# Turning the quantised 1024-wide activations by a DMA transpose in place of eight TensorE transposes and a ScalarE copy

## The reference

```
h  = layernorm(x);  q = h Wq;  k, v = split(concat(ctx, h) Wkv)     # 16 heads of 16, 1101 keys
x1 = x + softmax(mask(q k^T / 4)) v Wout + bout                      # query i sees keys up to i + 77
g  = layernorm(x1)
a  = gelu(quant(g) quant(w_fc)^T + b_fc)                             # 256 -> 1024
out = x1 + quant(a) quant(w_proj)^T + b_proj                         # 1024 -> 256
```

## Time and profile before

| | |
|---|---|
| Median of 3 runs | 743.06 us (741.91 to 748.08) |
| Profiled execution, its own time | 746.14 us |
| Its span, first to last instruction | 744.4 us |
| Mean granted clock of PE, of full speed | 0.924 |
| PE / ACT / DVE / POOL busy | 615.4 / 461.5 / 417.2 / 209.3 us |
| 16 DMA engines, hardware queue | 42.6% of the span, 42.63 MB |

### The profile page before, as it was taken

The page is one execution under the profiler, slowest core; times in us unless marked ns, Lnnn a source line. Parts: engine busy times, 40 slices in busy tenths (PEclk is TensorE's granted clock), DMA queues, the critical chain, the costliest instruction groups (busy, mean ns, idle before and its releaser), DMA issues.

```text
span 744.4 us, 11509 instructions
## 1 busy us (share of the span) xinstructions
PE 615.4 (83%) x4031; PEld 260.7 (35%) x4040; DVE 417.2 (56%) x888; ACT 461.5 (62%) x612; POOL 209.3 (28%) x272
## 2 busy tenths in 40 slices
PE   3668876869989888798899879898899879998365
PEld 2333323223345324323444324333344324233223
DVE  3321567685643846827654756537426658572664
ACT  2335745457855677587765775587775767888022
POOL 2202322142122541232423532133331532232100
PEclk9969979799999999999999999899999999999756
DMA  5495691444039590207239570108069540100000
GB/s 141 52 110 112 73 145 13 146 50 44 1 49 121 67 94 22 90 2 80 41 46 109 74 66 16 44 1 92 30 67 111 77 39 17 44 3 29 0 0 29
DMA packets 43911, 43.64 MB, mean 59 GB/s; under 512 B 3979, under 2 KB 43527, under 8 KB 43834
## 3 DMA queue, kind: packets, MB, share of 16 engines
q1 hardware_dynamic: 43834, 42.63, 42.6%
HBM read 12.12 MB, written 4.19 MB: 22 GB/s over the span
## 4 chain that ended last, share of the span: by engine, by line
PE 64%; ACT 14%; DVE 10%; issue 8%; DMA 2%; SPq 1%; DVEq 0%; POOL 0%; ACTq 0%
PE psO L1166 18%; PE psS L1181 14%; ACT probs L662 9%; PE psD L1044 9%; PE psD L1054 5%; PE psD L1078 4%; PE psD L1113 4%; PE psD L1098 4%; PE psD L1096 2%; PE psD L1104 2%; ACT hT L692 1%; DMA k_stack<-k_parts 1%; DVE amax L813 1%; DVE stats L776 1%; DVE hid L824 1%
## 5 line engine op out<-in xcount | busy, mean ns | idle before, releaser
L662 ACT ACTIVATE probs<-psS 128x1024 f32<-128x1024 f32 (+3 forms) x384 | 330.6, 909 | 190.9 <-PE psS L1181 190.1
L1181 PE MATMUL psS<-q_stack,k_stack 99*128 99x512 bf16 (+4 forms) x896 | 198.6, 334 | 47.6 <-ACT probs L662 43.4
L607 POOL TENSOR_SCALAR_AFFINE_SELECT probs<-probs 128x512 f32<-128x512 f32 (+2 forms) x160 | 109.6, 696 | 333.4 <-ACT probs L662 333.3
L1166 PE MATMUL psO<-probs,v_aug 128*17 128x512 f32 (+4 forms) x1792 | 182.6, 506 | 1.1 <-issue 0.8
L1181 PEld LDWEIGHTS psS<-q_stack,k_stack 99*128 99x128 bf16 (+1 forms) x896 | 70.6, 103 | 168.0 <-ACT probs L662 116.7
L1166 PEld LDWEIGHTS psO<-probs,v_aug 128*17 128x17 f32 (+1 forms) x1792 | 37.3, 98 | 93.7 <-issue 82.0
L813 DVE TENSOR_REDUCE amax<-hid 128x32 f32<-128x1024 f32 x44 | 53.3, 1210 | 29.2 <-ACT hid L747 28.6
L939 DVE STREAM_TRANSPOSE o_cols<-psO 128x512 f32<-128x512 f32 x32 | 22.9, 717 | 75.1 <-PE psO L1166 74.8
L747 ACT ACTIVATE hid<-psD 128x512 f32<-128x512 f32 x64 | 36.8, 597 | 40.7 <-PE psD L1098 40.5
L824 DVE TENSOR_TENSOR hid<-hid,magic 128x1024 f32<-128x1024 f32 x44 | 56.9, 1292 | 4.6 <-issue 3.8
L825 DVE TENSOR_TENSOR hq<-hid,magic 128x1024 bf16<-128x1024 f32 x40 | 54.6, 1366 | 1.4
(11 more groups left out here) (88 smaller groups left out, 584.0 us busy)
## 6 DMA issues: line engine op xcount, KB each, us to landing
q_stack<-q_parts SPq DMA_DIRECT2D x96, 128.0 KB, 8.3
k_stack<-k_parts SPq DMA_DIRECT2D x48, 147.2 KB, 8.4
k_stack<-k_parts SPq DMA_DIRECT2D x48, 128.0 KB, 9.5
x_in<-in_x_dram SPq DMA_DIRECT2D x8, 512.0 KB, 6.5
x<-in_x_dram SPq DMA_DIRECT2D x8, 512.0 KB, 8.7
out_dram<-x SPq DMA_DIRECT2D x16, 256.0 KB, 2.2
hid<-in_L_ffn_w_fc_dram SPq DMA_DIRECT2D x1, 1024.0 KB, 14.4
hid<-in_L_ffn_w_proj_dram SPq DMA_DIRECT2D x1, 1024.0 KB, 5.0
```

Of the source, the lines that this page charges most:

```text
L607: last = pool.affine_select(out=tile, in_=tile, compare_op=ALU.is_ge, fill=0.0, base=first - (P * t - CTX), pattern=[[0, GH], [1, m]], cha ...
L662: act.activation(probs[:, k % PB, 2 * pair:2 * pair + 2, 0:n], psS[:, 2 * pair:2 * pair + 2, 0:n], ACT.Exp, scale=DH ** -0.5).then_inc(pro ...
L1166: last = pe.matmul(psO[SQ * j:SQ * j + VW, first - CHUNK * st.c:first - CHUNK * st.c + n], v_aug[0:rows, v_tile(st.b, st.c, t), GH * st.g ...
L1181: last = pe.matmul(psS[0:rows, j, off:off + n], k_stack[0:ROWS, GH * st.g + j, P * t:P * t + rows], q_heads(0, ROWS, st)[:, j, first - CHU ...
```

## The change

For each token tile the kernel no longer does the eight PE transposes and the ACT copy; SP issues one DMA transpose, 128x1024 bf16 from `hq[:, t % 2]` to `hT[:, t % 2]`, SBUF to SBUF. `hT` leaves `IN_BANK` and `BY_ACT`, so it takes no bank and the turns of the others shift. SP waits for `hq_ready`, and from the third tile on for PE having finished the `proj` that read the buffer. The waits of DVE's `hq` and PE's `proj` on the turned tile become waits on the DMA's semaphore (`turned`). In the bursts `hT` is placed a half or a whole slot after its `hq` (some a slot earlier than before), and the second `proj` of most bursts a slot later. The context load, until now inside `xin` and so waiting for `ctxT` of the batch before, becomes an item of its own, `cin`, at slot -42.

```
--- before.py
+++ after.py
@@ -172,6 +172,7 @@
         if b:
             put(b, (-45, -68, -81)[b - 1], "xin", b, 0)
             put(b, (-44.5, -67.5, -80.5)[b - 1], "xin", b, 1)
+            put(b, -42, "cin", b)
             for c, places in enumerate((((-35, -34, -33), (-32, -30, -29)), ((-65, -63, -61), ), ((-54, -52, -51), ))[b - 1]):
                 for s, kind in zip(places, ("ln1", "ln1root", "ln1end")):
                     put(b, s, kind, b, c)
@@ -209,11 +210,11 @@
                 put(b, s, kind, b, c)
             series(b, [places[2] + 1 + t for t in range(SUB)], "x1b", b, SUB * c)
         if not b:
-            burst(put, b, 0, 36, (39, 40, 42, 43, 44, 45, 46, 47), (41.5, 43.5, 46.5, 48.5), (46, 49.5))
+            burst(put, b, 0, 36, (39, 40, 42, 43, 44, 45, 46, 47), (40.5, 43.5, 46.5, 47.5), (46, 49.5))
         else:
-            burst(put, b, 0, 28, (31, 32, 34, 35, 36, 37, 38, 39), (33.5, 36.5, 38.5, 40.5), (38, 42))
+            burst(put, b, 0, 28, (31, 32, 34, 35, 36, 37, 38, 39), (32.5, 35.5, 38.5, 39.5), (38, 43))
         if b < B - 1:
-            burst(put, b, 1, PER_BATCH + 11, (14, 15, 16, 18, 19, 20, 21, 22), (16.5, 19.5, 21.5, 23.5), (21, 25))
+            burst(put, b, 1, PER_BATCH + 11, (14, 15, 16, 18, 19, 20, 21, 22), (15.5, 18.5, 21.5, 22.5), (21, 26))
     for i in range(2):
         for h in range(2):
             put(0, 21 + 9 * i + 2 * h - i * h, "wquant", i, h)
@@ -251,8 +252,8 @@
 
 PLAN = plan()
 ORDER = [it for k in range(-1, TOTAL + 1) for h in (0, 1) for it in PLAN[k, h]]
-IN_BANK = ("wout", "xqT", "fc", "hT", "proj", "ctxT", "xnT", "qk", "v", "flag", "wT")
-BY_ACT = ("ctxT", "xnT", "v", "hT")
+IN_BANK = ("wout", "xqT", "fc", "proj", "ctxT", "xnT", "qk", "v", "flag", "wT")
+BY_ACT = ("ctxT", "xnT", "v")
 
 
 def act_plan():
@@ -419,6 +420,7 @@
         x1_read = sem("x1_read")
         x1_biased = sem("x1_biased")
         xq_ready = sem("xq_ready")
+        hT_loaded = [sem("hT_loaded0"), sem("hT_loaded1")]
         hq_ready = sem("hq_ready")
         y_stored = [sem(f"y_stored{i}") for i in range(CHUNKS)]
 
@@ -443,6 +445,11 @@
 
             n, used = BANK[item]
             return bank_free[n], used + 1
+
+        def turned(item):
+
+
+            return hT_loaded[item[-1] % 2], 16 * (NUMBER[item] // 2 + 1)
 
         def flag_of(eng, b, c):
 
@@ -546,9 +553,10 @@
                         b, c = item[1:]
                         sp.wait_ge(*taken(("xnT", b - 1, 2 * c + 1)))
                         load_x(b, c)
-                        if c == 0:
-                            sp.wait_ge(*taken(("ctxT", b - 1)))
-                            load(ctx_rows[:, :], ctx_in[b], ctx_loaded)
+                    if kind == "cin":
+                        b = item[1]
+                        sp.wait_ge(*taken(("ctxT", b - 1)))
+                        load(ctx_rows[:, :], ctx_in[b], ctx_loaded)
                     if kind == "xres":
                         b, c = item[1:]
                         if b:
@@ -564,6 +572,15 @@
                         sp.wait_ge(w_taken, 2)
                         load(w_rows.rearrange("p (t k) -> p t k", k=HID),
                              w_proj.rearrange("(t p) k -> p t k", p=P), fcw_loaded)
+                    if kind == "hT":
+                        b, t = item[1:]
+                        number = NUMBER[item]
+                        sp.wait_ge(hq_ready, number + 1)
+                        if number >= 2:
+                            before = ("proj", TILES[number - 2][1], TILES[number - 2][2] // 2)
+                            n, used = BANK[before]
+                            sp.wait_ge(bank_full[n], used + 1)
+                        sp.dma_start_transpose(hT[:, t % 2, :, :], hq[:, t % 2, :]).then_inc(hT_loaded[t % 2], 16)
                     if kind == "proj":
                         b, p = item[1:]
                         sp.wait_ge(*taken(item))
@@ -684,12 +701,6 @@
                     tile, rows = (v_tile(b, 0, SUB), LAST_KEYS) if t == 4 else (v_tile(b, 1, 2 * t), P)
                     last = act.copy(v_aug[0:rows, tile:tile + 2, :, 0:DH],
                                     ps[0:rows, :].rearrange("p (a h d) -> p a h d", a=2, d=DH))
-                if kind == "hT":
-                    number = NUMBER[item]
-                    if number >= 2:
-                        _, bb, tt = TILES[number - 2]
-                        act.wait_ge(*taken(("proj", bb, tt // 2)))
-                    last = act.copy(hT[:, t % 2, :, :].rearrange("p k n -> p (k n)"), ps[:, :].bitcast(BF16))
                 last.then_inc(bank_free[n], 1)
 
             def parts_places(item):
@@ -984,7 +995,7 @@
                     b, t = item[1:]
                     number = NUMBER[item]
                     if number >= 2:
-                        dve.wait_ge(*taken(TILES[number - 2]))
+                        dve.wait_ge(*turned(TILES[number - 2]))
                     round_off(hid[:, t % SUB, :], hq[:, t % 2, :], HID, dve_hq, 4 * number).then_inc(hq_ready, 1)
                 if kind == "proj":
                     b, p = item[1:]
@@ -1097,18 +1108,12 @@
                     for kk in range(KD):
                         last = pe.matmul(ps[:, :], xqT[:, t % SUB, kk, :], wfc[:, kk, cols],
                                          start=False, stop=(kk == KD - 1))
-                if kind == "hT":
-                    t = item[-1]
-                    pe.wait_ge(hq_ready, NUMBER[item] + 1)
-                    for kk in range(KH):
-                        last = pe.transpose(ps[:, kk * P // 2:(kk + 1) * P // 2].bitcast(BF16),
-                                            hq[:, t % 2, kk * P:(kk + 1) * P], ident_b[:, :])
                 if kind == "proj":
                     b, p = item[1:]
                     if NUMBER[item] == 0:
                         pe.wait_ge(*taken(("wT", 1, 3)))
                     for t in (2 * p, 2 * p + 1):
-                        pe.wait_ge(*taken(("hT", b, t)))
+                        pe.wait_ge(*turned(("hT", b, t)))
                         for kk in range(KH):
                             last = pe.matmul(ps[:, D * (t % 2):D * (t % 2 + 1)], hT[:, t % 2, kk, :], wproj[:, kk, :],
                                              start=(kk == 0), stop=(kk == KH - 1))
```

30 lines of the change are left out of this document (20 added, 10 removed).

## The result

| | before | changed kernel |
|---|---|---|
| Median (lowest to highest), 4 runs each | 744.15 us (741.91 to 748.08) | 756.15 us (751.35 to 759.8) |
| Profiled execution, its span | 744.4 us | 749.6 us |
| Mean granted clock of PE | 0.924 | 0.914 |

The ratio is 1.0144 (95%: 1.0084 to 1.0204): the changed kernel is 1.4% slower, where 0.8% faster was forecast. Now and then an execution of any kernel is longer at a lower clock; ratios and their intervals leave such executions out and medians do not, so where the two differ the ratio decides. The time lies inside the range given, on the wrong side of the forecast. Its profiled execution is its fastest one (751.35 us), so the profile shows 5.2 of the 12.0 us by which the medians differ; a second profile of the same kernel, in the experiments, is a typical one.

What follows compares the result with a forecast made beforehand. Beside attention, PE and its hand-over to ACT were taken to bound the kernel; -15.4 + 10.7 - 0.9 = -5.6 us made 746.1 into 740.5, or 737.5 against the median of 743.1; range 721 to 762.

Steps and rivals of the forecast that it cites:

- first batch, PE waits behind the stack: Fourth tile's transpose queues behind slot 47's 12 copies, landing at 235.8; second half of `proj` waits: 5.7 us lost.
- second and third batch: Second tile's transpose stands behind the stack of slot 32.5, so `proj` waits: 2.5 us lost in each batch.
- after attention: Last four tiles, one behind the other: the last transpose lands at 737.9 where the copy ended at 738.7; 0.9 us off.
- 22 tiles at 0.70, all other slots: Tiles beside attention, outside the stalled stretches, each save 0.70 us of PE transposes and ACT copy: 15.4 us off.
- the three places: First, second and third batch, where a stack stands ahead of a transpose in SP's queue: 10.7 us lost in all.
- The rival of a slow transpose: Each transpose takes 9.5 us, like a copy in a stack, and PE waits at `proj`: 770 us; chance 0.22.
- the second rule: Skill's rule that transposing DMAs are about as fast as plain ones; said to put the sum near -11 us.
- I take 0.70, since PE's own saving is nearly that and does not need ACT's: Gain per tile beside attention, from chain shares of the transposes and copy; chosen between ends of 0.42 and 0.89 us.
- PE's time is not worth that much: Rival: only 0.42 us a tile gained beside attention, other late work taking over; +0.6 us, 743.7 us; chance 0.20.
- the first stall: First batch, slot 47.5 transpose behind the stack: landing at 235.8 against `proj`'s second half at 230.1, 5.7 us lost.

Runs made afterwards that it cites:

- both edits: Changed kernel with slot 47's stack issued half a slot later and the second and third batch's slot 32.5 stacks three slots later: 0.9886, 739.42 us; again 0.9907, 744.12 us.
- the filler: Kernel with both stack moves, plus eight PE transposes of a constant per tile into a bank nobody reads: ratio 0.9986 to the kernel before, 747.38 us.
- the other: Changed kernel with only the stacks of slot 32.5 in the second and third batch issued three slots later: ratio 1.0064 to the kernel before, 751.51 us.

## Why the prediction was wrong

Its own sum, term by term, against the first profile (us; the row of the 22 tiles is what is left when the others are taken from 5.2):

```
                                         predicted   measured
first batch, PE waits behind the stack      +5.7       +9.5
second and third batch                      +5.0       +5.7
after attention                             -0.9       -0.6
22 tiles at 0.70, all other slots          -15.4       -8.4
slots before the first tile                  0         -1.0
sum                                         -5.6       +5.2
```

**Right: the landing and the three places.** 3.1 us a transpose against 2.9 (the 230 GB/s that one of its bounds gives a store is in no row: a store alone moves its 256 KB in 0.9 us in the trace of before, some 290 GB/s, which leaves 1.3 us fixed and not 1.1); waits at the slots named and nowhere else beside attention; the first landing at 237.1 against 235.8; the end shorter by 0.3 us from the second tile's `hq` (0.6 from the last slot), where 0.9 were predicted: the last `hq` follows 0.8 us earlier, not 1.5. That this decides the sign is shown, by the edits that move only the stacks: 1.6% slower becomes 1.1% faster. The rival of a slow transpose is refuted by its landing time. Of the two rules weighed, the Trainium skill's "VectorE: DVE Perf Modes", The three transpose paths, gives 1309 ns for a block by DMA; eight blocks in 3.1 us are 0.39 us each, so that figure does not add up over a tile. The Trainium skill's "Advanced Engine Details and Errata", X-Bar Transpose (TRN2), that a transposing DMA is as fast as a plain one, comes nearer: 3.1 us here beside the 2.2 of a store of the same size. What the prediction made of the second rule is a slip: 2.2 in place of 2.9 us, five times, takes 3.5 us off -5.6, which is -9.1 and not near -11.

**Wrong: the step "I take 0.70, since PE's own saving is nearly that and does not need ACT's".** What it measured is 0.38 us a tile, near the 0.42 of the rival "PE's time is not worth that much". That 0.38 is a remainder of one profile; the second profile gives 0.30, and the kernel with both edits, in which PE hardly waits for a transpose, gains 3.7 and 5.1 us in its two profiles over all 28 tiles beside attention, 0.13 and 0.18 a tile. Three readings say why. First, the shares of the chain do not add: without the copy 9.4 us go, and with both removed 8.8 go, in a prediction that summed 13.4 and 10.4. Second, PE's own saving is not nearly that: with the copy gone already, 21.6 us of PE work are worth 5.9, 0.18 us a tile. That PE is often about to wait for an exponential anyway (41.5 us of waits for L679 after the change) would fit, but is argued. Whether PE's saving needs ACT's is open, for no run takes PE's part away and keeps the copy. It was the copy, the smaller number in the chain, that was worth nearly its full 10.4. Third, what PE gains beside attention is partly given back at places with nothing of the change in them: slots 96 to 111, ahead of the first transpose of their burst, lose 2.0 us. The chain there, from 405 to 416 us in order of time, shows a wait that nothing releases:

```profile
410.99 0.47 PE psO L1171 x8
411.46 1.71 PE psD L1065 x7
413.17 1.61 issue
414.79 0.38 PE psD L1065
```

Such "issue" waits, 1.6 to 3.9 us, near 255 us and between 400 and 435, appear in the kernels whose PE has no transposes in its instruction stream, even where no DMA turns anything, and in none of the four where PE still transposes `hq`; the one with the filler has a single one, elsewhere (1.84 us, before 364). The traces show what PE waits for. Part 3 of the page counts the packets that bring instructions; for the changed kernel:

```profile
q8 instruction: 44, 0.72, 0.5%
```

These are 44 packets of 16 KB, and 46 in the kernels whose PE transposes, so they carry PE's stream. Set beside the waits (worked out from the packets in the traces), all 26 "issue" waits of PE of over 0.7 us in the fourteen traces end 1.2 to 2.1 us after such a packet has come in, while these packets come some 16 us apart. The waits also stand at fixed places of the stream: those near 415 us after 4,220 instructions in four traces, those near 255 after 2,413 or 2,414 in four. So PE stands because its next instructions have not come yet. That taking the transposes out matters because it moves other instructions onto the ends of the packets is argued, and why one packet comes late and the next in time is open: the one at 413 falls where a stack holds the rings (DMA share 1.14 to 1.15 from 405 to 417 us) and took 1.9 us, but as long ones pass elsewhere without a wait. The clock adds to it: at half clock between 190 and 690 us are 27.3 us before, 41.0 and 44.4 in the two profiles after, 30.7 without the copy, 34.1 and 37.5 with both edits. Where such a stretch begins, the slot is 1.64 us longer. Why it begins where it does is open; the run with the filler speaks against the missing transposes.

**Too small: the first stall.** I priced the wait at the landing less the old start of `proj`, 5.7 us. The wait ended 1.3 us later than predicted, and PE worked at half clock from 237.1 to about 241.6; half of those 4.5 us is the loss, an estimate of 2.3. Together 9.3 of the 9.5. In the other two places, with under 2 us of wait, 2.8 us each were lost where 2.5 were predicted (slots 32 to 40 of the batch, from the same comparison); but in the second batch 1.64 of it is a stretch at half clock in slot 83, ahead of the wait, which stands just so in the kernel without that wait ("the other"). The wait itself cost 2.1 us there (slot 87: +2.4 with it, +0.3 without), so that 2.8 comes near 2.5 is in part luck.

**The medians.** They put 12 us where the profile has 5. The second profile of the changed kernel, equal to its median, has +10.9 with the same waits, to within 0.2 us; it is longer ahead of slot 28 and in slots 140 to 160. A single profile of a kernel whose runs spread over 8 us should not be read to 5 us, and I predicted a median from one.

**Still open:** why each edit of the stack alone brings so much less by the medians than both; why some packets of instructions come late; where ACT's time goes when it issues the transposes.

## What to carry to other kernels

A transfer that an in-order engine waits for belongs ahead of bulk copies in whatever queue issues it: list, for each such transfer, what is in the rings when it is issued, and how soon it is needed, for the place can cost more than the transfer does (11.0 us in place of 3.1 here). Price the wait with the slow clock that follows it. And read a line's share of the chain as the most that its removal can bring, not as what it brings: here two neighbouring lines that alternate in the chain were worth about one of them.

## What the runs showed of the hardware

- A DMA transpose of 128x1024 bf16 from SBUF to SBUF lands in 3.0 to 3.1 us on free rings and holds the issuing engine 1.25 us, twice a plain issue (0.6). A second one, issued while the first still stands behind a stack, held SP for 5.2 to 7.2 us (kernels with the stacks of slot 32.5 moved).
- It moves in small packets: those under 512 B rise from 3,979 to 37,771, some 1,056 a transpose; with no DMA issued for the turning they are 3,979 again.
- Issued right behind 12 copies of a stack it takes 10.9 to 11.4 us on SP's queue and 11.8 to 11.9 on ACT's, and on ACT's 8.3 with three of them ahead. Issued with the first copy by ACT it takes 5.6 to 5.9 us; by SP ahead of it, 3.0.
- PE can stand 0.8 to 3.9 us with every semaphore given, in kernels of one form at the same instruction of its stream; all 26 such waits ended 1.2 to 2.1 us after a 16 KB packet of instructions came in.
- After a 9.6 us wait the granted clock stayed at 1.2 GHz for some 4.5 us of work.
